# Two layer 1 blocks and the mixing coefficients loaded on their own, and one warm-up product fewer

## What is computed

```python
x = x + L0(x, cond, W_base, b_base, As, Bs)         # adapters: x W_base' + b + 2 * sum_e cond[b,e] (x As_e') Bs_e'
x = x + L1(x, cond, weight, mask, bias)             # w_bot[b] = sum_g cond[b,g] * weight[g] * mask;  x w_bot[b]' + bias
x = x + L2(x, cond, skill_*, shared_*)              # top 2 of softmax(cond) pick expert MLPs (gelu), plus one shared MLP
x = x + L3(x, cond, W_up, b_up, W_gate, ..)         # argmax(cond) picks one expert: silu(up) * gate, down
```

## Time and profile before

| what | value |
|---|---|
| median of the runs | 86.51 us |
| the profiled execution's own time | 87.03 us |
| its span, first to last instruction | 85.2 us |
| TensorE, matmuls (share of the span) | 82.0 us (96%) |
| VectorE / ScalarE / GpSimd | 48.5 (57%) / 31.7 (37%) / 15.8 (19%) us |
| moved by DMA | 18.51 MB, mean 217 GB/s |

### The profile page before, as it was taken

One profiled execution on the slowest core, in us unless ns is written; L12 is line 12 of the kernel. 1 busy time (PEld: TensorE's weight loads), 2 busy tenths in 40 slices (PEclk: granted clock), 3 DMA queues, 4 the chain that ended last, 5 costly groups with the idle time before them and its releaser, 6 DMA issues.

```text
span 85.2 us, 1938 instructions
## 1 busy us (share of the span) xinstructions
PE 82.0 (96%) x620; PEld 77.6 (91%) x620; DVE 48.5 (57%) x115; ACT 31.7 (37%) x59; POOL 15.8 (19%) x20
## 2 busy tenths in 40 slices
PE   6999999999999999999999999999999999999980
PEld 6879998888889989999999999999999999999960
DVE  1487798845336996446438428438446555463170
ACT  6502795875558401123121221221212302407450
POOL 3020298389666700000000000000000000000000
DMA  1995000699990001884879899988899898607002
GB/s 15 387 388 221 0 0 0 211 415 400 421 382 28 0 0 14 309 250 190 314 245 328 253 308 323 302 277 294 265 331 314 289 315 330 251 35 205 11 0 65
DMA packets 5336, 18.51 MB, mean 217 GB/s; under 512 B 592, under 2 KB 1744, under 8 KB 5328
## 3 DMA queue, kind: packets, MB, share of 16 engines
q1 hardware_dynamic: 5040, 17.62, 59.8%
q10 hardware_dynamic: 288, 0.79, 2.4%
HBM read 17.88 MB, written 0.52 MB: 216 GB/s over the span
## 4 chain that ended last, share of the span: by engine, by line
PE 96%; DVE 0%; issue 0%; DVEq 0%
PE bank L687 34%; PE bank L697 17%; PE bank L710 8%; PE bank L724 4%; PE bank L651 4%; PE bank L659 4%; PE bank L667 4%; PE bank L589 4%; PE bank L583 3%; PE bank L674 2%; PE bank L675 2%; PE bank L677 2%; PE bank L607 2%; PE bank L619 2%; PE bank L598 2%; DVE out_sb L504 0%
## 5 line engine op out<-in xcount | busy, mean ns | idle before, releaser
L687 PE MATMUL bank<-x_t,pair_w 128*128 128x128 f32 (+1 forms) x256 | 31.2, 276 | 0.0
L687 PEld LDWEIGHTS bank<-x_t,pair_w 128*128 128x128 f32 x256 | 29.9, 192 | 0.3
L298 ACT ACTIVATE gelu<-bank 128x512 f32<-128x512 f32 x24 | 14.2, 596 | 32.2 <-PE bank L687 28.2
L475 DVE SCALAR_TENSOR_TENSOR hid<-gelu,wsel,bank 128x512 f32<-128x512 f32 x16 | 12.0, 748 | 18.9 <-PE bank L687 18.8
L697 PE MATMUL bank<-hid,pair_w 128*128 128x128 f32 x128 | 16.9, 275 | 0.0
L697 PEld LDWEIGHTS bank<-hid,pair_w 128*128 128x128 f32 x128 | 15.6, 192 | 0.1
L262 POOL TENSOR_TENSOR hid_l<-hid,hid_h 128x512 fp32r<-128x512 f32 x8 | 10.2, 1286 | 4.3 <-ACT hid_h L326 4.3
L473 DVE TENSOR_TENSOR hid<-gelu,bank 128x512 f32<-128x512 f32 x8 | 5.5, 688 | 6.3 <-ACT gelu L298 3.8
L710 PE MATMUL bank<-x_t,w 128*128 128x128 f32 x64 | 8.5, 276 | 0.0
L710 PEld LDWEIGHTS bank<-x_t,w 128*128 128x128 f32 x64 | 7.8, 192 | 0.0
L302 ACT ACTIVATE tanh<-half 128x256 f32<-128x256 f32 x6 | 2.5, 416 | 10.1 <-DVE half L511 10.1
(11 more groups left out here) (70 smaller groups left out, 77.4 us busy)
## 6 DMA issues: line engine op xcount, KB each, us to landing
pair_w<-in_skill SPq DMA_DIRECT2D x16, 768.0 KB, 5.5
w<-in_layer SPq DMA_DIRECT2D x8, 384.0 KB, 5.5
rest_sb<-in_rest SPq DMA_DIRECT2D x1, 661.0 KB, 3.9
x_t<-in_x SPq DMA_DIRECT2D x1, 512.0 KB, 4.8
shared_sb<-in_shared ACTq DMA_DIRECT2D x1, 512.0 KB, 4.5
out_x<-out_sb SPq DMA_DIRECT2D x8, 64.0 KB, 4.4
shared_sb<-in_shared ACTq DMA_DIRECT2D x1, 256.0 KB, 4.8
head_sb<-in_head SPq DMA_DIRECT2D x1, 164.0 KB, 2.4
```

The costliest lines, as they stand in the source:

```text
L298: act.activation(gelu[:, n, :], ps[:, :], ACT.Gelu_apprx_tanh).then_inc(gelu_ready, 1)
L475: dve.scalar_tensor_tensor(hid[:, n, :], gelu[:, n, :], wsel[:, bass.DynSlice(weight, 1)], u_ps[n][:, :], ALU.mult, ALU.mult).then_inc(hid ...
L687: mm = pe.matmul(ps[:, S * t:S * (t + 1)], pair_w[:, slot, n, 128 * t:128 * (t + 1)], x2_t[:, columns(b)], start=True, stop=True)
```

## The change

A part of two transfers travels apart. The first two of the eight layer 1 blocks leave `rest` and become `first`, the first transfer on SyncE's queue. The coefficients `wcol` leave `head` and become `coef`, 8 floats on each partition, the first thing that ScalarE's queue does. VectorE writes `mix1` ahead of its `b_mix` steps, and TensorE starts with the two early blocks, then does `mix0`, then the six other blocks. The warm-up has 5 products in place of 6. Shapes, sums and everything from `product0` on are the same.

```diff
-HEAD = 2 * C + B + B * E
+HEAD = 2 * C + B * E
+EARLY = 2
...
-WARM = 6
+WARM = 5
...
+        wcol = sb("wcol", [128, B])
+        first_sb = sb("first_sb", [128, EARLY * C])
...
-        rest_sb = sb("rest_sb", [128, REST + OL * C])
+        rest_sb = sb("rest_sb", [128, REST + (OL - EARLY) * C])
...
         def _(sp):
+            sp.dma_start(first_sb[:, :], first[:, :]).then_inc(first_in, 16)
             sp.dma_start(head_sb[:, :], head[:, :]).then_inc(head_in, 16)
...
         def _(act):
+            act.dma_start(wcol[:, :], coef[:, :]).then_inc(coef_in, 16)
             act.preload_act_table(ACT.Exp)
+            act.wait_ge(coef_in, 16)
             act.wait_ge(head_in, 16)
...
+            dve.wait_ge(coef_in, 16)
+            dve.tensor_tensor(mix1[:, :].rearrange("p (b o) -> p b o", o=OH), delta[:, :].unsqueeze(1).broadcast_to([128, B, OH]),
+                              wcol[:, :].unsqueeze(2).broadcast_to([128, B, OH]), ALU.mult).then_inc(mix1_ready, 1)
             dve.wait_ge(head_in, 16)
             for b in range(HALF):
                 dve.tensor_scalar(b_mix[:, b, :], b_sb, wcol[:, b:b + 1], None, ALU.mult).then_inc(b_mixed, 1)
-            dve.tensor_tensor(mix1[:, :].rearrange("p (b o) -> p b o", o=OH), delta[:, :].unsqueeze(1).broadcast_to([128, B, OH]),
-                              wcol.unsqueeze(2).broadcast_to([128, B, OH]), ALU.mult).then_inc(mix1_ready, 1)
...
+                    weights = (first_sb[:, C * a:C * (a + 1)] if a < EARLY else
+                               rest_sb[:, REST + C * (a - EARLY):REST + C * (a - EARLY + 1)])
+                    mm = pe.matmul(bank[5 + h][:, 128 * n:128 * (n + 1)], weights, mix1[:, :], start=True, stop=True)
...
+            pe.wait_ge(first_in, 16)
+            pe.wait_ge(mix1_ready, 1)
+            mix1_part(0, EARLY)
             pe.wait_ge(head_in, 16)
             mix0(0, 1, b_mixed, 1)
             mix0(1, 2, b_mixed, 2)
             mix0(2, HALF, b_mixed, HALF)
             mix0(HALF, B, b_mixed2, HALF)
             pe.wait_ge(rest_landed, 16)
-            pe.wait_ge(mix1_ready, 1)
-            mix1_part(0, OL)
+            mix1_part(EARLY, OL)
```

More of the change, by code:

```diff
@@ L28, with build @@
 REST = sum(_WIDTHS)
-WARM = 6
-def build(nc, x, head, rest_in, shared, skill, layer3, out):
+WARM = 5
+def build(nc, x, coef, first, head, rest_in, shared, skill, layer3, out):
     fp32, fp32r, i32 = mybir.dt.float32, mybir.dt.float32r, mybir.dt.int32
@@ L74, in build @@
         head_sb = sb("head_sb", [128, HEAD])
-        a_sb, b_sb, wcol = head_sb[:, 0:C], head_sb[:, C:2 * C], head_sb[:, 2 * C:2 * C + B]
-        condb = head_sb[:, 2 * C + B:HEAD]
+        a_sb, b_sb, condb = head_sb[:, 0:C], head_sb[:, C:2 * C], head_sb[:, 2 * C:HEAD]
+        wcol = sb("wcol", [128, B])
+        first_sb = sb("first_sb", [128, EARLY * C])
         delta = sb("delta", [128, OH])
         mix1 = sb("mix1", [128, B * OH])
-        rest_sb = sb("rest_sb", [128, REST + OL * C])
+        rest_sb = sb("rest_sb", [128, REST + (OL - EARLY) * C])
         base_t, mask_t, b0col, b1col, bias3 = (rest_sb[:, at:at + n] for at, n in REST_PARTS)
@@ L126, in build @@
         head_in, rest_landed = sem("head_in"), sem("rest_landed")
-        x_loaded = sem("x_loaded")
+        first_in, coef_in, x_loaded = sem("first_in"), sem("coef_in"), sem("x_loaded")
         mix1_ready = sem("mix1_ready")
@@ L597, in mix1_part @@
                     h, n = a // (OL // 2), a % (OL // 2)
-                    mm = pe.matmul(bank[5 + h][:, 128 * n:128 * (n + 1)], rest_sb[:, REST + C * a:REST + C * (a + 1)], mix1[:, :], start=True, stop=True)
+                    weights = (first_sb[:, C * a:C * (a + 1)] if a < EARLY else
+                               rest_sb[:, REST + C * (a - EARLY):REST + C * (a - EARLY + 1)])
+                    mm = pe.matmul(bank[5 + h][:, 128 * n:128 * (n + 1)], weights, mix1[:, :], start=True, stop=True)
                     if n == OL // 2 - 1:
@@ L812 @@
         "in_x": of("x").transpose(2, 0, 1).reshape(C, B * S),
+        "in_coef": _np.repeat(cond.T, R, axis=0),
+        "in_first": weight1[:, :EARLY * C],
         "in_head": _np.concatenate([of("L0_cond_As").reshape(128, C), _np.swapaxes(of("L0_cond_Bs"), 1, 2).reshape(128, C),
-                                    _np.repeat(cond.T, R, axis=0), _np.repeat(cond.reshape(1, B * E), 128, axis=0)], axis=1),
+                                    _np.repeat(cond.reshape(1, B * E), 128, axis=0)], axis=1),
         "in_rest": _np.concatenate([
@@ L817 @@
             of("L0_cond_b_base").reshape(C, 1), of("L1_cond_bias").reshape(C, 1),
-            bias3.transpose(2, 1, 0).reshape(128, -1), weight1], axis=1),
+            bias3.transpose(2, 1, 0).reshape(128, -1), weight1[:, EARLY * C:]], axis=1),
         "in_shared": gated(of("L2_cond_shared_gate"), of("L2_cond_shared_up"), of("L2_cond_shared_down")),
```

## The result

The changed kernel takes **87.09 us** (median of 22 runs, 86.68 to 87.65); the kernel before, run beside it, 86.80 us (22 runs, 85.75 to 88.36). The ratio is **1.0082, 95% interval 1.0059 to 1.0105**: by the ratio slower by 0.5 to 0.9 us, where 0.2 us of gain was forecast; 87.09 lies above the range. The lower edge moved, from 85.75 to 86.68; the upper one didn't rise. The base was low as well: the 86.51 of three runs became 86.80 with 22.

The account below looks back on a forecast made before the run. TensorE was taken to bound the kernel. Useful work starting 0.41 us earlier at half clock brings the first product of x from 8.38 to 8.16 us, gain 0.22; from base 86.51 that gives 86.3 us, range 85.8 to 86.9.

Parts of the forecast that it names:

- Bytes, not issues, set its end: Load of the rest: issued 0.48 us later but 131 KB shorter, so landing moves from 5.07 to 5.1 to 5.3 us.
- ScalarE ... sits idle 0.75 us between the two: Shared weights issued 0.44 us later; idle time between ScalarE's rounding and its bias step at 9.09 us was to hide it.
- cover: Work that must stay hidden; for VectorE's routing, if cover failed, each 0.1 us late would cost 0.1 us.
- The start of useful work: TensorE's first block weight load at 3.21 us, 0.41 us earlier than before, with `coef` taking 2.0 us to land.
- the gain of 0.22: First product of x at 8.16 us in place of 8.38, since useful work starts 0.41 us earlier at half speed.
- The base: Median of 86.51 us for the kernel before, from which the gain was subtracted to forecast 86.3 us.
- if it keeps its moment: TensorE's clock was taken to rise from 1.2 to 2.4 GHz at 5.99 us, as before the change.
- the prediction's own signs of being wrong: First block after 3.5 us, clock's rise moved over 0.4 us, or first product of x early without the end.
- rival 3: Longer idle between zeros and first block delays the clock's rise to 8.4 us, costing 1.2 us: 87.7 us; chance 0.07.
- Rival 2: Small `coef` rows are slow or something behind absorbs the gain: 86.5 to 87.0 us; chance 0.22.

Follow-up runs that it names:

- e8: Kernel before with only the two early blocks split off, ahead of the adapter matrices; old engine order, six products of zeros: ratio 1.0084 (1.0036 to 1.0131).
- e14: Kernel before with only the two early blocks split off, issued behind the adapter matrices; old engine order: ratio 1.0059 (1.0014 to 1.0104).
- e7: Kernel before with only the coefficients as a transfer of their own; blocks together, old engine order, six products of zeros: ratio 1.0027 (0.9974 to 1.0080).
- e5: Changed kernel with the arrays in memory laid out as before, early blocks and coefficients still transferred separately: ratio 1.0110 (1.0072 to 1.0148).
- e9: As e8, but the rest travels in rows of 5288 bytes, carrying the two blocks again unread: two runs, 86.96 and 88.95 us.
- e1: The changed kernel once more, nothing altered: 87.11 us, ratio 1.0103 (1.0060 to 1.0146) to the kernel before.
- e6: Changed kernel with ScalarE's rounding of the first shared weight moved behind the second bias step of layer 0: ratio 1.0073 (1.0023 to 1.0124).
- e13: Changed kernel with six products of zeros and the early blocks issued on ScalarE's queue ahead of the coefficients: four runs, 87.67 to 89.62 us.
- e3: Kernel before with five products of zeros in place of six, nothing else changed: ratio 1.0041 (1.0003 to 1.0080).
- e2: Changed kernel with six products of zeros again, as before the change: ratio 1.0104 (1.0062 to 1.0146).
- e4: Changed kernel's split transfers alone, with the kernel before's order of work on TensorE and VectorE and six products of zeros: ratio 1.0083 (1.0050 to 1.0116).
- e18: Changed kernel, ScalarE's queue issuing coefficients, then early blocks; seven products of zeros, rounding behind the second bias step: ratio 1.0158 (1.0081 to 1.0235).
- e11: Kernel before with seven products of zeros in place of six: ratio 1.0004 (0.9966 to 1.0043).

## Why the prediction was wrong

- **"Bytes, not issues, set its end"** is the step that failed: the rest landed at about 6.3 us, not 5.1 to 5.3, since the reads fell to 142 GB/s with the engines busy. e8 and e14 have the dip with the blocks' transfer alone and e7 doesn't have it with the coefficients' alone; e5 and e9 show that the memory layout and the row length don't make it.
- **"ScalarE ... sits idle 0.75 us between the two"** failed with it: a delay was counted only as the 0.44 us of a later issue, and the rounding came 1.37 us later (9.08 for 7.71). e1 and e6 show that the bias steps, and through them the layer 1 products, wait for it. I had listed the wait as cover and asked what it would cost only for VectorE's.
- The start of useful work: 3.54, forecast 3.21. `coef` took 2.31 us for 2.0, inside the bounds, and that is nearly all of the 0.33; TensorE began 0.12 us behind `mix1`, as said. The start gave 0.08 us in place of 0.41, so of the gain of 0.22 no more than 0.04 was there to be had. `first` took 2.1 us (forecast 2.3) and `head` 2.3 (2.4), and `mix0` found its data.
- The base: 86.51 was the median of three runs, 86.80 is that of 22. Of the 0.79 us between the forecast of 86.3 and the measured 87.09, 0.29 is that and no part of the mechanism.
- The clock "if it keeps its moment": it doesn't, in any kernel. It moved between 4.5 and 6.5 us for the same code (e1 and the first profile). Two of the prediction's own signs of being wrong came about: the clock's rise moved by 0.52 us, over 0.4, and the first block started at 3.57, after 3.5. The mechanism of rival 3 is seen in e13, at 2.5 us of idle, and e3 gives the shorter warm-up a cost of 0.03 to 0.7 us in the kernel before. In the changed kernel it isn't the main cause: e2 undid it and gained nothing that its runs can show, and e4 has the loss with six zeros.
- Rival 2, something behind that absorbs the gain, was the right kind with too low a price: it was bounded by "86.5 to 87.0", from a gain lost, and not from loads that all come later. The trace of before had most of the numbers for it: with 1.14 us from the rounding to the layer 1 products they could start at 7.71 + 1.14 = 8.85 and did at 10.16, so 1.31 us was to spare in that execution. A delay of 1.37 uses it up, and in an execution whose clock rises earlier there is less to spare.
- What is shown of the cause: the blocks' transfer of its own costs time (e4, e8 and, with useful work starting as before, e14: 1.0083, 1.0084, 1.0059), and the late shared load is a floor under the lowest times. What isn't: how much of the mean the floor makes. e6 took the wait away and its ratio hardly moved; a second wait, for x, came up, and the rise of the clock differs from run to run. Why the rate falls is open too.

## What to carry to other kernels

Before you add a transfer to a stream of loads that keeps the engines full, list for each later load who waits for it first and with how much slack, down to the engine stream in which a step that isn't urgent stands ahead of one that is. Read the rate beside the busy share: engines that are 97% busy moved 142 GB/s. And where a time spreads over more than a microsecond, compare the edges of the spread, not one profile: a floor shows in the lower edge. Take the base from as many runs, too: three were 0.29 us off here.

## What the runs showed of the hardware

- A 131 KB transfer in rows of 1 KB on SyncE's queue was followed by 0.5 to 1 us in which the reads ran at 73 to 257 GB/s in place of about 390, in ten profiles of eleven; in the changed kernel eleven packets of the next transfer took 0.5 to 1.37 us each, where 0.17 is the median. What does it stays open. Tried and excluded: array layout, row length of the rest, its place ahead of the adapter matrices, the moment of x's issue.
- A small transfer on ScalarE's queue, beside large ones on SyncE's, could land as late as the large one: 128 KB after 4.4 us in e18 (3.1 in e13, first on its queue), and 4 KB, behind 128 KB, after 4.2 us in e13. Alone at the head of its queue, 4 KB in rows of 32 bytes took 2.2 to 2.5 us.
- A load is landed when its last packet is: in e11 reads at 385 to 406 GB/s from 5 to 7.5 us, and then a tail of 25 and 16 GB/s from 8 us on, put the shared weights 0.89 us later than in the kernel before, with the same transfers.
- The clock rose anywhere from 3.76 to 9.15 us after the start, at 4.54 and 6.50 in two executions of the same kernel; the granted clock column read 1.00 throughout.
